# The score matmuls of two heads alternate by row half in a fusion layer on one Trainium2 core

## What is computed

```python
h = concat(tok(x), txt)                                  # 8 x 548 x 192
q, k, v = (layernorm(h) @ W.T for W in (Wq, Wk, Wv))     # 3 heads of 64
scores = einsum('blhe,bmhe->bhlm', q, k) / 8 * decay     # gamma[h] ** (m - l), 0 where m < l
weights = softmax(scores, axis=-1)                       # zeros of the decay take part
o = einsum('bhlm,bmhe->blhe', weights, v)
h = h + (groupnorm(o) * gn_weight + gn_bias) @ Wo.T
logits = layernorm(h) @ router_w.T                       # top 8 of 16 experts
h = h + sum_e comb[:, e] * (gelu(x2 @ w1[e]) @ w2[e])
```

## Time and profile before

| | us |
|---|---|
| median of 3 runs (lowest, highest) | 893.6 (891.85, 896.51) |
| the profiled execution's own time | 896.59 |
| its span | 894.8 |
| TensorE matmul busy in the span | 832.1 |
| VectorE busy | 575.7 |
| ScalarE busy | 494.3 |
| POOL busy | 88.7 |

### The profile page before, as it was taken

The page is one execution under the profiler, slowest core; times in us unless marked ns, Lnnn a source line. Parts: engine busy times, 40 slices in busy tenths (PEclk is TensorE's granted clock), DMA queues, the critical chain, the costliest instruction groups (busy, mean ns, idle before and its releaser), DMA issues.

```text
span 894.8 us, 18021 instructions
## 1 busy us (share of the span) xinstructions
PE 832.1 (93%) x6048; PEld 770.4 (86%) x6048; DVE 575.7 (64%) x1558; ACT 494.3 (55%) x1102; POOL 88.7 (10%) x164
## 2 busy tenths in 40 slices
PE   5779999999999995779999999999999999999996
PEld 2757878797887874579999999999999999999996
DVE  6647788888888774585565555655655655655554
ACT  1357778887787884434444444444444444444443
POOL 3111030220203011160000000000000000000000
PEclk9779999999999997679999999999999999999999
DMA  8300010101101027422532232232232322322320
GB/s 236 118 18 19 1 57 2 55 2 57 44 13 55 2 75 274 150 77 64 167 106 74 65 90 79 63 88 81 75 75 80 89 63 76 103 71 63 93 65 20
DMA packets 34421, 67.30 MB, mean 75 GB/s; under 512 B 3632, under 2 KB 14160, under 8 KB 34256
## 3 DMA queue, kind: packets, MB, share of 16 engines
q1 hardware_dynamic: 34384, 66.84, 25.2%
HBM read 55.41 MB, written 11.42 MB: 75 GB/s over the span
## 4 chain that ended last, share of the span: by engine, by line
PE 69%; issue 16%; DVE 4%; POOL 3%; ACT 3%; POOLq 3%; DMA 0%; ACTq 0%; DVEq 0%; SPq 0%
PE ps L1085 64%; PE ps L1223 2%; ACT xn L473 2%; POOL w_lo L403 2%; POOLq L380 1%; PE ps L1123 1%; POOLq L413 1%; DVE out_r L1049 1%; PE ps L1440 1%; ACT pt L460 1%; PE ps L1441 0%; DVE w_lo L796 0%; PE ps L1302 0%; DMA x_dram<-y 0%; DVE sc L841 0%
## 5 line engine op out<-in xcount | busy, mean ns | idle before, releaser
L1031 DVE TENSOR_TENSOR act<-act,gate 128x548 f32<-128x548 f32 x192 | 141.0, 738 | 202.9 <-ACT act L682 202.9
L682 ACT ACTIVATE act<-ps 128x548 f32<-128x548 f32 x192 | 120.5, 628 | 247.9 <-PE ps L1085 245.3
L1085 PE MATMUL ps<-x_all,w_hi 128*128 (+1 forms) x1152 | 252.9, 292 | 1.2 <-ACT act L682 1.2
L1085 PE MATMUL ps<-x_all,w_lo 128*128 (+1 forms) x768 | 216.6, 291 | 0.0
L1085 PEld LDWEIGHTS ps<-x_all,w_hi 128*128 128x128 f32 x1152 | 195.2, 190 | 1.5 <-SPq L236 1.4
L1085 PEld LDWEIGHTS ps<-x_all,w_lo 128*128 128x128 f32 x768 | 146.3, 191 | 0.0
L796 DVE TENSOR_TENSOR act_lo<-act,act_hi 128x548 fp32r<-128x548 f32 x192 | 141.6, 738 | 1.3
L460 ACT ACTIVATE act_hi<-act 128x548 fp32r<-128x548 f32 x192 | 125.7, 655 | 19.4 <-DVE act L1031 19.4
L1085 PE MATMUL ps<-act_hi,w_hi 128*128 128x274 f32 x384 | 112.9, 294 | 6.4 <-DVE act_lo L796 4.1
L1085 PE MATMUL ps<-act_hi,w_lo 128*128 128x274 f32 x384 | 111.9, 291 | 0.0
L1085 PE MATMUL ps<-act_lo,w_hi 128*128 128x274 f32 x384 | 111.7, 291 | 0.0
(11 more groups left out here) (189 smaller groups left out, 1314.7 us busy)
## 6 DMA issues: line engine op xcount, KB each, us to landing
gate<-comb_dram SPq DMA_DIRECT2D x128, 274.0 KB, 3.3
x_all<-x_dram SPq DMA_DIRECT2D x8, 822.0 KB, 4.9
x_dram<-x SPq DMA_DIRECT2D x7, 822.0 KB, 3.5
w_raw<-w SPq DMA_DIRECT2D x8, 384.0 KB, 3.5
out<-h SPq DMA_DIRECT2D x8, 384.0 KB
w_others<-w SPq DMA_DIRECT2D x1, 2304.0 KB, 10.4
h<-txt SPq DMA_DIRECT2D x3, 672.0 KB
decay_rows<-drow SPq DMA_DIRECT2D x1, 1014.0 KB, 8.9
```

The lines of the kernel that those rows point to most:

```text
L682: a.activation(act[k % 3][:, :, :], ps[:, 2 * (k % 2):2 * (k % 2) + 2, 0:HALF], ACT.Gelu_apprx_tanh).then_inc(gelu_done, 1)
L1031: dve.tensor_tensor(act[k % 3][:, :, :], act[k % 3][:, :, :], gate[e % 4][:, :, :], ALU.mult).then_inc(gated, 1)
L1085: return pe.matmul(dst, w, x, start=start, stop=stop)
```

## The change

The three score groups are written anew. `scores_first` computes tile 0 of heads 0 and 1, `scores_rest` their tiles 1 to 4, `scores_third` head 2. In the first two, head 0's and head 1's matmuls alternate, so that each follows one on the other half of the partitions, and the heads write different banks:

| tile | head 0 before | head 1 before | head 0 now | head 1 now |
|---|---|---|---|---|
| 0 | banks 0, 1 | banks 0, 1 | banks 0, 1 | banks 2, 3 |
| 1 | bank 2 | bank 2 | bank 0 | bank 1 |
| 2 to 4 | bank 3 | bank 3 | bank 2 | bank 3 |

The number of matmuls and their shapes are the same. VectorE's decay follows: `decay_first` takes both tiles 0, `decay_rest` both tiles 1 and then tiles 2 to 4 of head 0 and of head 1, `decay_third` head 2. ScalarE's order is unchanged; the counts that it waits for are.

```diff
--- before.py
+++ after.py
@@ exps
                     if I == 0:
-                        a.wait_ge(nm_ready, nth(b, 2 * H, 2 * hh + 1))
+                        a.wait_ge(nm_ready, nth(b, 2 * H, (1, 2, 5)[hh]))
                     elif I == 1:
-                        a.wait_ge(nm_ready, nth(b, 2 * H, 2 * hh + 2))
+                        a.wait_ge(nm_ready, nth(b, 2 * H, (3, 4, 6)[hh]))
@@ vector
+            def decay_first(b):
+                dve.wait_ge(s_done, nth(b, 6, 1))
+                apart(dve, "dve")
+                for hh in range(2):
+                    decay_tile(hh, 0, ps[:, 2 * hh:2 * hh + 2, 0:HALF])
+                    negate_max(hh, slice(0, 1))
+
+            def decay_rest(b):
+                dve.wait_ge(s_done, nth(b, 6, 2))
+                apart(dve, "dve")
+                for hh in range(2):
+                    decay_tile(hh, 1, ps[:, hh, 0:L - P])
+                dve.wait_ge(s_done, nth(b, 6, 3))
+                apart(dve, "dve")
+                for hh in range(2):
+                    for I in range(2, NT):
+                        decay_tile(hh, I, ps[:rows(I), 2 + hh, S_AT[I]:S_AT[I] + L - P * I])
+                    negate_max(hh, slice(1, NT))
...
-                apply_decay(b, 0)
+                decay_first(b)
                 if more:
                     norm_stats(b + 1, st6, mv, veps, ln1_var)
-                apply_decay(b, 1)
+                decay_rest(b)
                 normalise(b, 0)
@@ tensor
+            def score_pair(parts):
+
+                pairs = ((q01_hi, k01_hi), (q01_hi, k01_lo), (q01_lo, k01_hi))
+                for i, (a_, b_) in enumerate(pairs):
+                    for hh, bank, at, I, m0, m1 in parts:
+                        g = slice(HD * hh, HD * hh + HD)
+                        q = slice(I * P, I * P + rows(I))
+                        last = mm(ps[:rows(I), bank, at:at + m1 - m0], a_[g, q], b_[g, m0:m1], i == 0, i == len(pairs) - 1)
+                return last
+
+            def scores_first(b):
+                pe.wait_ge(qk_lo, nth(b, 4, 4))
+                for n in range(2):
+                    last = score_pair([(hh, 2 * hh + n, 0, 0, n * HALF, (n + 1) * HALF) for hh in range(2)])
+                last.then_inc(s_done, 1)
+
+            def scores_rest(b):
+
+                pe.wait_ge(decayed, nth(b, NT * H, 1))
+                score_pair([(hh, hh, 0, 1, P, L) for hh in range(2)]).then_inc(s_done, 1)
+                pe.wait_ge(decayed, nth(b, NT * H, 2))
+                for I in range(2, NT):
+                    last = score_pair([(hh, 2 + hh, S_AT[I], I, I * P, L) for hh in range(2)])
+                last.then_inc(s_done, 1)
...
@@ body, tensor
-                scores(b, 0, tail, router)
+                scores_first(b)
                 if tail:
                     probs_transpose(t, 2, (2, 3))
                     pe.wait_ge(qk_lo, nth(b, 4, 1))
                     attend(t, 2)
-                scores(b, 1, tail, router)
+                scores_rest(b)
```

More of the change, by code:

```diff
@@ L825, in qk_rest, with decay_tile @@
                     sub(two(dst[p0:P, :]), halves(bank, p0), two(hi[p0:P, :])).then_inc(qk_lo, 1)
-            def apply_decay(b, hh):
+            def decay_tile(hh, I, src):
                 s = hh % 2
+                r, n = rows(I), L - P * I
+                dst, tab = sc[s][:r, OFF[I]:OFF[I] + n], decay[:r, hh, 0:n]
+                if I == 0:
+                    dst, tab = two(dst), two(tab)
+                dve.tensor_tensor_reduce(out=dst, in0=src, in1=tab, scale=1.0 / 8, scalar=0.0 if I else NEG,
+                                         op0=ALU.mult, op1=ALU.max,
+                                         accum_out=mx[s][:r, I:I + 1]).then_inc(decayed, 1)
@@ L837, in apply_decay @@
                     elif I == 1:
-                        src = ps[:, 2, 0:n]
+                        decay_tile(2, I, ps[:, 2, 0:L - P])
                     else:
[L840 to L847, removed]
+                        decay_tile(2, I, ps[:rows(I), 3, S_AT[I]:S_AT[I] + L - P * I])
+                negate_max(2, slice(1, NT))
             def normalise(b, hh):
@@ L1160, in values, with score_tile @@
                         last.then_inc(v_done, 1)
[L1162 to L1167, removed]
[L1168 to L1180 removed]
+            def score_tile(dst, pairs, g, I, m0, m1):
+                q = slice(I * P, I * P + rows(I))
+                return series(dst, [(a_[g, q], b_[g, m0:m1]) for a_, b_ in pairs])
@@ new lines, in scores_third @@
+            def scores_third(b, tail, router):
+                pairs = ((q2, k2_hi), (q2, k2_lo))
+                g = slice(0, P)
+                for I in range(NT):
+                    if I <= 2:
+                        pe.wait_ge(decayed, nth(b, NT * H, (PAIR_I1, PAIR_0, PAIR_1)[I]))
+                    if I == 1 and router:
+                        pe.wait_ge(l_sub, nth(b - 2, 1, 1))
+                    if I == 1 and tail:
+                        pe.wait_ge(gn_var, nth(b - 1, 1, 1))
+                    if I == 2:
+                        pe.wait_ge(v_copied, nth(b, 3, 3))
@@ L1181, in scores @@
                     r, n = rows(I), L - P * I
[L1182 removed]
                     if I == 0:
[L1184 removed]
+                        score_tile(ps[:, 0, 0:HALF], pairs, g, I, 0, HALF)
+                        last = score_tile(ps[:, 1, 0:HALF], pairs, g, I, HALF, L)
                     elif I == 1:
[L1186 removed]
+                        last = score_tile(ps[:, 2, 0:n], pairs, g, I, P, L)
@@ L1187, in scores @@
                     else:
-                        parts = [(ps[:r, 3, S_AT[I]:S_AT[I] + n], I * P, L)]
-                    for dst, m0, m1 in parts:
-                        last = series(dst, [(a_[g, q], b_[g, m0:m1]) for a_, b_ in pairs])
+                        last = score_tile(ps[:r, 3, S_AT[I]:S_AT[I] + n], pairs, g, I, I * P, L)
                     if I in (0, 1, 4):
@@ L1339, in body @@
                 probs_transpose(b, 1, (0, 1))
-                scores(b, 2, tail, router)
+                scores_third(b, tail, router)
                 probs_transpose(b, 1, (2, 3))
```

39 lines of the change are left out of this document (15 added, 24 removed).

## The result

The changed kernel takes **906.98 us** (median of 6 runs, 905.41 to 907.77), the kernel before 893.74 us in the same comparison (6 runs): a ratio of 1.0134, 95% interval 1.0114 to 1.0154. It is slower by 13 us, and the number forecast was 906.4. The sum behind that number is a different matter: its terms did not all come out as written, and the rest of this document is about that.

The account below looks back on a forecast made before the run. TensorE, though 93% busy, was taken as released by VectorE, which waits for ScalarE. 1.49 us lost at the logits copy plus 0.1 for POOL, 1.6 a body, times eight is 12.8 on the 893.6 median: 906.4 us, range 894 to 914.

Parts of the forecast that it names:

- The first group waits for more: TensorE's first score group: waits for the fourth q/k remainder, so begins at 150.73 in place of 149.86, 0.87 us later.
- Pace: Score matmuls of two row halves on TensorE: taken at 0.11 us per matmul, between full overlap and none.
- Weight loads one by one: Forecast's case for score pairs: matmuls overlap, weight loads pass one after another, 0.11 us per matmul; chance 0.42, 906.4 us.
- the full-overlap rival: Score pairs on TensorE cost one matmul; 0.3 us lost a body, 0.4 with the negation slowed by POOL; 896.8 us, chance 0.31.
- VectorE's order: Head 0's second negation comes behind previous attention, statistics and head 1's tiles 0 and 1; ScalarE gets it 2.9 us later.
- the forecast's own case: Score pairs with weight loads passing one by one, 0.11 us per matmul; 1.6 us lost a body, 906.4 us, chance 0.42.
- The finish line: ScalarE's logits copy at 166.94: its 8.23 us block would end at 168.43, using the 1.43 idle and losing 1.49 us.
- The collision: Head 0's second negation on VectorE moves to where POOL splits w1; could lose 0 to 0.5 us, 0.1 taken.
- Every body like the others: All eight attention bodies, including the first two without the router, priced alike at 1.6 us each: 12.8 us.
- The clock: TensorE idles 2 us or so before head 0's probabilities, dropping its clock: at least 2 us more a body; 922, chance 0.07.
- the pace's two ends: Score pairs on TensorE: price of one matmul (896.8 us, chance 0.31) or of two (912.0 us, chance 0.12).

Follow-up runs that it names:

- section 3: Kernel before the change, with one wait moved: head 0's token tile 0 waits for the fourth q/k remainder instead of the third; 902.13 us, ratio 1.0074.
- the filled kernel: Changed kernel plus 12 unread 274-column matmuls behind the value matmuls, where TensorE waits 1.59 us; 900.46 us, ratio 1.0061.
- the kernel of section 2: Changed kernel with each group's matmuls reordered, e.g. all six of head 0's tile 0, then all six of head 1's; 916.67 us, ratio 1.0235.
- 5, with its control: Changed kernel with 12 unread matmuls behind the values, 900.46 us; control: kernel before with six in the same place, 894.73 us, ratio 0.9993.
- 4: Two runs on the changed kernel: ScalarE's first head 1 exponential moved ahead of head 0's tiles 1 to 4, 902.51 us; VectorE's second group head 0 first, 901.05 us.
- the gated kernel: Kernel before the change, with only head 0's tile 0 wait moved from the third to the fourth q/k remainder; 902.13 us, ratio 1.0074.
- section 1: Changed kernel with, within each step, head 0's three score matmuls issued before head 1's three instead of alternating; 906.9 us, ratio 1.0132.

## Why the prediction was right, and where it was not

The total, 906.4, is 0.6 us from the measurement. It was not earned term by term. The direction was, and so was the mechanism up to the logits copy; the size of a body and the way from one body to eight were not.

**The first group waits for more: held.** The first score matmul stands at 153.74, 0.06 us behind the end of the fourth remainder (152.95 + 0.73). The size was 0.87 on TensorE; alone in the old order it makes a body 0.64 longer (section 3). The prediction let the nine larger matmuls that left the group pay for it and looked no further. That the clock can fall behind this idle stretch was not in it. Nor was the start of the kernel, where the gate is worth 1.3 us once.

**Pace: this is the step that failed.** "Weight loads one by one", 0.11 us a matmul, made a pair 0.22. It measured 0.13 a pair for 274 columns: the matmuls and weight loads of the two halves run fully side by side. The two 164-column rows showed the limit of weight loads *into the same rows*, and I carried it over to different rows, of which no row told anything. The Trainium skill, TensorEngine Tiling (Array Packing), § Tiling Modes, had it right. By this the steady body at full clock should follow the full-overlap rival, 0.4 us longer. It was 0.15 longer.

**VectorE's order: held, a third smaller.** ScalarE was to wait 2.9 us for head 0's second negation; it waits 2.03 (1.7 to 3.6 was named as the mark). With the overlap partly undone it waits 3.4 and a body at full clock takes 40.67 us, 1.5 above: that is the forecast's own case, in the kernel it would have fitted.

**The finish line: the mechanism held, the size came from the pace.** ScalarE's block was summed at 8.23 us and takes 8.14, and at full clock the 1.43 idle before the logits copy is used up, as forecast. What was off is when the block starts: the negation was put 10.3 us behind the start of the fourth remainder (160.2 less 149.88), and in the third body it is 9.3 behind it (122.97 less 113.66). That 1.0 us is most of what lies between the 1.49 forecast and the 0.15 measured. In the bodies at 0.96, ScalarE does wait for the logits (1.25 us in the fourth), because TensorE computes them at half clock. TensorE's wait ahead of the probabilities was put at 2 us or so, and measured 1.59, with a second one of 0.75 for v, which the sum did not have.

**The collision: about right in size, with another operation.** The negation took 0.40 us, not 0.17; 0.2 lost where 0.1 was taken. It ends at 162.24, as POOL's cast ahead of the w1 split does (line 400, to 162.20); the split itself, line 403, starts at 162.42.

```profile
161.25 0.95 POOL L400 CAST w_hi<-w_raw 128x384 f32 x2
```

**Every body like the others: wrong.** The 1.6 us a body is close to what the fourth lost (1.54), but only by agreement of two different things. The bodies lost -0.28 to 2.33; the stretch before the first differs by 1.68, of which the gate's wait is 1.3, and the last one, the eighth body with the drain, by 1.77, of which no run shows how much is the change's. The second body, without the router's work, has nothing else for TensorE to do, which is where waiting for probabilities hurts (3.20 us, and 1.07 for v before) and the clock falls to 0.96 over the body.

**The clock: a rival with a chance of 0.07 that came true in part.** Its mechanism is the one seen: TensorE idles about 2 us ahead of head 0's probabilities, and the clock falls. It happened in three of the steady bodies and the second, not in each, and cost 1.0 to 1.4 us, not 2 or more. The filled kernel is 6.5 us of the 13.2 faster; 3.5 of them are seen as clock kept in the steady bodies.

So the match is an accident. Pairs faster than forecast left 0.15 us of the 1.6 in a steady body. Of the 9.7 us between the two profiled spans, 3.6 are clock in the fourth to sixth body (40.69, 40.55 and 40.27 against 39.30), 2.3 the second body, 1.7 the start and 1.8 the last stretch; the 3.5 us that the traces don't have come on top. The range, 894 to 914, held because it spanned the pace's two ends. The prediction also weighed "full overlap" as hardly a loss (896.8); even with its pace confirmed, that case came to 907. The fault was to treat pace and clock as exclusive. With its pairs side by side TensorE saves 2.1 us in a body and waits 2.25 us more, and the clock can be lost in those waits. It isn't the overlap itself that costs clock: in the kernel of section 2, with less of it, TensorE waits longer ahead of the transposes (2.57 us in the third body) and has a clock under 1.00 in four of five steady bodies.

Shown are the gate (section 3), the value of overlap as a lower bound (2), the clock of the steady bodies (5, with its control) and the negation's place (4). They do not add up to the whole and shouldn't: each repair also changes where TensorE idles. Why the clock falls in the fourth to sixth body and not in the third and seventh, which run the same instructions with the same waits, is open. So is why the first body takes about 34 us in some kernels and 37 in others, and what of the start and of the last stretch belongs to the change.

## What to carry to other kernels

When an edit lets the bounding engine do its work faster without moving what releases it, look for the idle stretch that this opens, and price what runs behind that stretch at the lower clock too. Ask of each wait that is moved forward how long the engine stands still in front of it: in the gated kernel 0.73 us cost 0.64, and 2.4 more in the bodies where the clock fell behind it. When two readings of an unknown cost lie a factor of two apart, don't let a row about one resource (weights into the same rows) settle a question about another.

## What the hardware showed that was not expected

- **The two row halves run at the same time, matmuls and weight loads alike, and within a short reach without regard to program order.** Three matmuls on rows 0 to 63 followed by three on rows 64 to 127 ran as three pairs (0.13 us each); six followed by six overlapped by three, and took 1.33 us where alternation takes 0.96. The page TensorE: Matmul & The Clock Gate of the Trainium skill, § The mechanism, says that matmuls start and end in program order; the starts at 155.13 and 155.37 of section 1 don't agree with that, since the second matmul at 155.13 is the fourth in the program and the two at 155.37 include the second.
- **The clock can fall behind short waits.** Idle stretches of 1.59 and 0.75 us with four transposes between them were followed by 4 us at a mean of 0.57 in three of the changed kernel's five steady bodies. In two bodies of the gated kernel one of 0.73 us, behind eight transposes, was followed by 2.4 us of score matmuls at 1.00 and then by 7.52 us at 0.55, and in the other steady bodies by no fall. That the wait is behind the fall follows from the kernel before, which differs in that wait alone and keeps its clock in these bodies; how it works is not shown.
- **Work that nobody reads can pay**: 12 matmuls a body, 6.5 us gained, 3.5 of them seen as clock kept in the steady bodies; six in a kernel whose steady bodies hold their clock change nothing (0.9993).
